# A four-layer decoder megakernel: five edits to the order of work in five of its stages

## What is computed

```python
# layer 0 feed-forward: gated sum of experts, each with a second bias
y = sum_e comb[:, e] * (gelu(h @ fc1[e] + b1[e]) @ fc2[e] + b2[e])
# layer 1 feed-forward: experts 0 and 1 have W = W + A @ B for gate, up and down
y = sum_e wt[:, e] * ((silu(h @ Wg[e]) * (h @ Wu[e])) @ Wd[e])
# layer 2 cross attention: q = rope(h @ Wq @ w_kc_q) @ W_qr ..., 16 heads
# layer 2 feed-forward: each token goes through one of 32 masked ternary matrices
# layer 3 attention, 16 heads of 128 nope and 64 rotary dimensions
q = rms(h @ Wq_a) @ Wq_b;  q_rope = rope(q[..., 128:])
score = (q_nope @ (Wk^T latent) + q_rope @ k_rope) / sqrt(192) + causal
out = softmax(score) @ latent, then folded with Wkv_b's value part and Wo
```

## Time and profile before

| what | value |
|---|---|
| median of three runs | 1622.96 us |
| the profiled execution's own time | 1620.76 us |
| its span, first to last instruction | 1619.0 us |
| granted TensorE clock, mean | 0.915 |
| TensorE matmul busy | 1356.9 us (84%) |
| VectorE busy | 828.8 us (51%) |
| ScalarE, GpSimd busy | 527.8 us (33%), 262.5 us (16%) |
| layer 0 feed-forward, start | 352.9 us |
| layer 1 feed-forward, start | 636.7 us |
| layer 2 cross attention, feed-forward, start | 918.6 us, 1189.7 us |
| layer 3 attention, start | 1287.4 us |

### The profile page before, as it was taken

The page is one execution under the profiler, slowest core; times in us unless marked ns, Lnnn a source line. Parts: engine busy times, 40 slices in busy tenths (PEclk is TensorE's granted clock), DMA queues, the critical chain, the costliest instruction groups (busy, mean ns, idle before and its releaser), DMA issues. The chain is left out here.

```text
span 1619.0 us, 28010 instructions
## 1 busy us (share of the span) xinstructions
PE 1356.9 (84%) x11687; PEld 1035.0 (64%) x11705; DVE 828.8 (51%) x1530; ACT 527.8 (33%) x967; POOL 262.5 (16%) x219
## 2 busy tenths in 40 slices
PE   5768996989999979799968888999748578978888
PEld 2348994557867667688847666787647444547555
DVE  4844435553253642433428546777345359981552
ACT  1331223562334652312223411223414413442451
POOL 0143422000120000111010113333010113320200
PEclk9868998988999989899978899999878799899999
DMA  3000001126014001000092240000056200000000
GB/s 100 1 1 4 4 4 54 53 63 137 0 35 142 1 1 30 1 1 1 1 241 82 79 141 1 1 1 1 1 166 215 87 8 1 1 0 1 28 1 26
DMA packets 83468, 69.41 MB, mean 43 GB/s; under 512 B 23752, under 2 KB 81552, under 8 KB 83216
## 3 DMA queue, kind: packets, MB, share of 16 engines
q1 hardware_dynamic: 82576, 65.53, 14.1%
q0 software_dynamic: 768, 2.10, 0.4%
HBM read 55.29 MB, written 12.32 MB: 42 GB/s over the span
## 5 line engine op out<-in xcount | busy, mean ns | idle before, releaser
L1158 PE MATMUL ps<-fixed,work 128*128 128x256 f32 x384 | 92.7, 392 | 20.5 <-DVE weights L1188 18.7
L1702 PE MATMUL ps<-rounded 128*128 128x512 f32 x384 | 96.3, 408 | 9.4 <-POOL rounded L1725 6.1
L637 PE MATMUL ps<-work,weights 128*128 128x256 f32 x384 | 89.3, 395 | 7.4 <-ACT weights L656 7.4
L1158 PEld LDWEIGHTS ps<-fixed,work 128*128 128x128 f32 x384 | 71.5, 193 | 35.9 <-DVE weights L1188 25.1
L1702 PEld LDWEIGHTS ps<-rounded 128*128 128x128 f32 x384 | 74.0, 195 | 29.4 <-issue 9.6
L637 PEld LDWEIGHTS ps<-work,weights 128*128 128x128 f32 x384 | 75.9, 199 | 19.3 <-ACT weights L656 8.3
L1207 POOL TENSOR_TENSOR fixed<-fixed,weights 128x768 f32<-128x768 f32 x32 | 58.0, 1811 | 148.3 <-DVE weights L1188 148.3
L1386 PE MATMUL ps<-work,weights 96*128 96x512 f32 x128 | 65.8, 641 | 12.4 <-DVE work L1409 10.4
L1725 POOL TENSOR_TENSOR rounded<-weights,rounded 128x256 fp32r<-128x256 f32 x32 | 22.9, 735 | 276.8 <-ACT rounded L1729 276.8
L656 ACT COPY weights<-ps 64x512 f32<-64x512 f32 x96 | 55.6, 579 | 25.8 <-PE ps L615 24.1
L1630 DVE SCALAR_TENSOR_TENSOR fixed<-ps,work,fixed 128x256 f32<-128x256 f32 x64 | 28.0, 479 | 65.5 <-PE ps L1563 65.5
(11 more groups left out here) (447 smaller groups left out, 3044.4 us busy)
## 6 DMA issues: line engine op xcount, KB each, us to landing
weights<-in_L_ffn_masksT SPq DMA_DIRECT2D x32, 256.0 KB, 5.6
sorted_in<-work SPq DMA_DIRECT2D x1, 4992.0 KB, 16.8
work<-sorted_in SPq DMA_DIRECT2D x13, 384.0 KB, 3.9
sorted_out<-work SPq DMA_DIRECT2D x13, 384.0 KB, 2.8
weights<-in_L_ffn_fc_w SPq DMA_DIRECT2D x16, 256.0 KB
weights<-in_L_xattn_Wq SPq DMA_DIRECT2D x2, 2048.0 KB, 10.0
weights<-in_L_xattn_WoT SPq DMA_DIRECT2D x2, 2048.0 KB, 10.4
weights<-in_L_ffn_Wg SPq DMA_DIRECT2D x8, 256.0 KB, 5.7
```

The source lines that it names most:

```text
L637: last = nc.tensor.matmul(ps[:, (0, 1, 4, 5)[j // 2], (j % 2) * D:(j % 2 + 1) * D], t.ctxT[:, u, j * P:(j + 1) * P], t.pm[:, u, :], start= ...
L1158: last = nc.tensor.matmul(seen[:, a, :], qf[:, c, u, a, :], k.hT[:, c, part * D:(part + 1) * D], start=c == 0, stop=c == KC - 1)
L1702: last = nc.tensor.matmul(ps[:, 2 * (n % 2) + i, :], a[:, q % 2, i, c, :], b[:, c, half * BANK:(half + 1) * BANK], start=c == 0 and part = ...
```

## The change

1. `project` waits in parts: tile 0 for the first sine operation of unit v-1, tile 1 for nothing, tile 2 for all three. `first_products` alternates between the two heads of a pair, so that neighbouring products use other rows and columns of the array and another PSUM bank.
2. Layer 3 attention: a unit is half of the tokens of a pair of heads, 16 in all. The rotary rows of both heads are one projection to bank 0, the nope rows of both another to bank 1. VectorE does three operations per unit, on 128, 64 and 64 rows. GpSimd does four additions of 32 rows per unit, three of them to other partitions than they read, and waits also for ScalarE's copies. Lag 3. GpSimd sorts the rotary weights with four copies in block 1. Four more DMAs.
3. The folds of layer 3 attention move into the layer 2 feed-forward, between the ranks and the first sorted block, behind 36 `hold` matmuls and a wait for the next stage's weights. ScalarE does the copies. Ten `hold` matmuls take their place.
4. Layer 1 feed-forward: experts in the order 2 to 7, 0, 1. Low-rank products in two parts: 4 first, 8 behind the first expert's products. ScalarE waits for the additions only before the last four halves.
5. Layer 0 feed-forward: the transposes of `comb` and the biases come behind expert 1's first products.

```diff
 def first_products(g):
-    for i in range(4):
-        p, e = divmod(i, 2)
-        for rows, width, first, tile in (...):
+    for p in range(2):
+        for tile, apart, at_row, width, first in ((0, 64, 0, 64, 0), (1, 64, 0, 64, 96), (2, 32, 0, 32, 64), (2, 32, 64, 32, 160)):
+            for e in range(2):
+                r, to = slice(64 * e, 64 * e + 64), at_row + apart * e
...
 def project(pe, v):
-    if v:
-        pe.wait_ge(s["sined"], 3 * v)
     for a in range(3):
+        if v and a != 1:
+            pe.wait_ge(s["sined"], 3 * v - 2 if a == 0 else 3 * v)
...
 # layer 3 attention, block 1
+@block.gpsimd
+def _(pool):
+    pool.wait_ge(w.sem, w.loaded)
+    for e in range(2):
+        for n in range(2):
+            nc.gpsimd.tensor_copy(to[:, :, :, n, e, :], of[:, :, :, e, n, :]).then_inc(s["sorted"], 1)
 # block 2: the loop over four fold groups and its copies on ScalarE and VectorE are gone
+hold(k, 6, 10)
 # block 3
+def projected(pe, v, kind, made):
+    u, tok = place(v)
+    for a in range(2):
+        last = nc.tensor.matmul(ps[:, 1 - kind, :], (w.nope, rot)[kind][:, a, u, :], qnT[:, a, tok], start=a == 0, stop=a == 1)
+    last.then_inc(s[made], 1)
+def rotated_rows(pe, v):
+    if v:
+        pe.wait_ge(s["sined"], 2 * v)
+    projected(pe, v, 1, "r_proj")
+def other_rows(pe, v):
+    if v:
+        pe.wait_ge(s["q_top"], 2 * v)
+    projected(pe, v, 0, "n_proj")
+def act_q(act, v):
+    act.wait_ge(s["n_proj"], v + 1)
+    if u >= 2:
+        act.wait_ge(s["scored"], 2 * u - 2)
+    for e in range(2):
+        nc.scalar.copy(qb[0:64, 2 * (u % 2) + e, tok], ps[64 * e:64 * e + 64, 1, :]).then_inc(s["q_top"], 1)
+def dve_q(dve, v):
+    dve.wait_ge(s["r_proj"], v + 1)
+    if v >= 2:
+        dve.wait_ge(s["q_ready"], v - 1)
+    nc.vector.tensor_tensor(by_seq(cs[:, v % 2, :]), by_seq(ps[:, 0, :]), bc(w.ropeT[:, 0, :], 1, 8), ALU.mult).then_inc(s["cosed"], 1)
+    for to, of in ((slice(0, 64), slice(64, 128)), (slice(64, 128), slice(0, 64))):
+        nc.vector.tensor_tensor(by_seq(sn[to, v % 2, :]), by_seq(ps[of, 0, :]), bc(w.ropeT[of, 1, :], 1, 8), ALU.mult).then_inc(s["sined"], 1)
+# GpSimd, for v in range(NH): waits cosed v + 1, sined 2 * v + 2, q_top 2 * v + 2, then
+    for e in range(2):
+        for half in range(2):
+            made = slice(64 * half + 32 * e, 64 * half + 32 * e + 32)
+            last = nc.gpsimd.tensor_tensor(qb[64 + 32 * half:96 + 32 * half, 2 * (u % 2) + e, tok], cs[made, v % 2, :], sn[made, v % 2, :], ALU.add)
+    last.then_inc(s["q_ready"], 1)
+attend(..., {"pe": rotated_rows, "pe_b": other_rows, "act": none, "act_b": act_q, "dve": dve_q,
+             "ready": lambda h: 2 * (h // 2) + 2}, 192 ** -0.5, causal=k.causal, turned=False, lag=3)
...
 # layer 0 feed-forward
-                if e == 0:
+                if e == 1:
                     pe.wait_ge(s["comb"], 1)
...
 # layer 1 feed-forward
+    TURN, LOW = (2, 3, 4, 5, 6, 7, 0, 1), (0, 4, 12)
+            low_rank(0)
             pe.wait_ge(s["h_rest"], KC)
...
+                if e == 0:
+                    pe.wait_ge(s["lowed"], 2)
+                    low_rank(1)
+                if e == 1:
+                    pe.wait_ge(s["lowed"], 6)
...
 # layer 2 feed-forward, TensorE, behind the ranks; ScalarE copies nope and pm of each g
+            hold(k, 4, 36)
+            pe.wait_ge(k.next.sem, k.next.loaded)
+            for g in range(4):
+                fold_nope(g)
+                fold_out(g)
+            pe.wait_ge(s["noped"], 4)
+            pe.wait_ge(s["pms"], 4)
             turn(0)
```

More of the change, by code:

```diff
@@ L1219, in load_L3_attn @@
     d, eng, r = k.dram, k.nc.sync, w.region
-    w.nr = r.take(2, NH, P, rows=96)
+    w.nope = r.take(2, NH // 2, P, rows=96)
+    w.pm = r.take(NH // 2, D)
     w.all = r.take(KC, 384)
@@ L1226, in load_L3_attn @@
     w.wo = r.take(NH, D)
+    w.rot = r.take(2, NH, DH, rows=96)
     w.rope = k.fixed.take(2, DH)
@@ L1253, in stage_L3_attn @@
     qnT = k.work.take(2, TOK, rows=96)
+    rot = k.work.take(2, NH // 2, P, rows=96)
     ss = k.work.take(2, NT)
     rstd = k.work.take(2, NT)
-    qb = k.work.take(3, TOK)
+    qb = k.work.take(4, TOK)
     sn = k.work.take(2, BANK)
@@ L1261, in stage_L3_attn @@
     kr = qb[:, 2, :].rearrange("p (a d) -> p a d", d=DH)
-    with k.stage("lat", "sq", "mean", "std", "rstd", "qn", "km", "kvn", "kra", "krb") as (block, s):
+    with k.stage("sorted", "lat", "sq", "mean", "std", "rstd", "qn", "km", "kvn", "kra", "krb") as (block, s):
         @block.tensor
@@ L1306, in stage_L3_attn @@
     lat = qb[0:64, 1, :]
-    with k.stage("vzero", "t_qn", "t_km", "c_qn", "c_km", "c_lat", "t_kv", "nope", "noped", "pm", "pms", "kvs") as (block, s):
+    with k.stage("vzero", "t_qn", "t_km", "c_qn", "c_km", "c_lat", "t_kv", "kvs") as (block, s):
         @block.tensor
@@ L1375, in stage_L3_attn @@
     w.region.at = w.mark
[L1376 to L1384, removed]
-            for a in range(2):
-                last = nc.tensor.matmul(ps[:, v % 2, :], w.nr[:, a, h, :], qnT[:, a, tok], start=a == 0, stop=a == 1)
-            last.then_inc(s["q_proj"], 1)
-        def act_q(act, v):
[L1390 to L1393, removed]
-            nc.scalar.copy(qb[0:64, h % 3, (v % 2) * BANK:(v % 2 + 1) * BANK], ps[0:64, v % 2, :]).then_inc(s["q_top"], 1)
-        quarters = (slice(64, 96), slice(96, 128))
-        def dve_q(dve, v):
-            h = v // 2
-            dve.wait_ge(s["q_proj"], v + 1)
-            if h >= 3:
-                dve.wait_ge(s["scored"], h - 2)
-            nc.vector.tensor_tensor(qb[hi, h % 3, (v % 2) * BANK:(v % 2 + 1) * BANK].rearrange("p (b t) -> p b t", t=SEQ),
-                                    ps[hi, v % 2, :].rearrange("p (b t) -> p b t", t=SEQ), bc(w.ropeT[hi, 0, :], 1, 8),
-                                    ALU.mult).then_inc(s["cosed"], 1)
@@ L1925, in copy_turned @@
                 nc.scalar.copy(sortedT[:, b % TURNED].rearrange("p c t -> p (c t)"), ps[:, b % 4, 0:KC * P]).then_inc(s["sortedT"], 1)
+            for g in range(4):
+                act.wait_ge(s["nope"], g + 1)
+                nc.scalar.copy(k.next.nope[:, :, 2 * g:2 * g + 2, :],
+                               ps[0:96, 2 + g % 2, :].rearrange("p (a i d) -> p a i d", a=2, i=2)).then_inc(s["noped"], 1)
+                act.wait_ge(s["pm"], g + 1)
+                nc.scalar.copy(k.next.pm[:, 2 * g:2 * g + 2, :].rearrange("p a d -> p (a d)"), ps[:, g % 2, :]).then_inc(s["pms"], 1)
             copy_turned(0)
@@ L2948, in decoder @@
             start_loads(n + 1)
+            k.next = loads.get(n + 1)
             rounded = ROUNDED_COLS.get(layer, 0)
```

125 lines of the change are left out of this document (65 added, 60 removed).

## The result

The changed kernel takes 1583.25 us (median of four, 1579.01 to 1589.24) beside 1621.74 us for the kernel before on the same chip: a ratio of 0.9754, with a 95% interval of 0.9729 to 0.978. The forecast was 1572 in a range of 1560 to 1590. The profiled execution took 1586.03 us, with a span of 1583.5, so 35.5 us less than the span before; 50.2 were forecast.

What follows compares the result with a forecast made beforehand. In the two attention loops neither engine fills the time; TensorE waits for VectorE in layer 2, and VectorE is never idle in layer 3. Terms 5 + 9 + 16.5 + 8.2 + 0.7 + 4.8 + 6 = 50.2 gave 1572 us, range 1560 to 1590.

Steps and rivals of the forecast that it cites:

- The start-up step of 4.5 us: Layer 2's attention loop: with the wait split, a start-up unit takes 4.5 us instead of 5.42; six such units save 5.5.
- Afterwards GpSimd stands next in line: Layer 2's loop after start-up: GpSimd's addition (1.82 us) becomes the next wait, 10.25 us per head against 10.83.
- VectorE's share: Layer 3's loop: VectorE loses 4.22 us per head and gains 2.1, so busy time falls from 8.0 to 5.9.
- the addition's price: Layer 3's loop: a GpSimd addition of 32 rows to other partitions costs 1.26 us, following columns; bounds 1.0 and 2.5.
- an addition takes over 1.6 us: Layer 3's loop: a GpSimd addition above 1.6 us was named as a sign that the prediction is wrong.
- today the first four blocks run at 1.2 GHz: Layer 2's feed-forward: the sorted blocks' transposes would start 0.9 us late but run at 2.4 GHz, net gain 0.7.
- Rival (c): Layer 2's feed-forward: clock stays low over the holds, fold ends late, 6 to 9 us lost: 1580; chance 0.13.
- biases at 2.4 GHz 16 x 0.21 = 3.4: Layer 0's feed-forward: behind expert 1, the 16 bias passes run at full clock and take 3.4 us, ending at 375.8.
- the lower end: Layer 0's feed-forward: gain of only 3 us instead of 6 if the clock falls in the copy's gap.
- (a): Layer 3's loop: GpSimd's shifted additions cost 1.5 to 2.2 us each and bound it, 1577 to 1620; chance 0.11.
- VectorE's 127.55 us: Layer 3's loop: VectorE's busy time now, divided by 16 heads to give 8.0 us per head.
- 0.99 us "beside nothing": VectorE's normalising product: 0.99 us with nothing beside it, against 1.81 beside GpSimd's addition in layer 2's loop.

Runs made afterwards that it cites:

- the second profile: The changed kernel profiled again with no edit: ratio 0.9756 to the kernel before, its profiled execution 1575.21 us.
- the filled kernel: The changed kernel plus unread products in TensorE's gaps in both grouped attention stages and layer 0's feed-forward: 1576.35 us, ratio 0.970.

## Why the prediction came out as it did

The total lay in the range and 11 us above the forecast. The stretches of the parts gave nearly the forecast sum, in part by luck: part 1b gave 3.5 us more than its term and part 5 3.5 less. By its steps:

- **Part 1a** (5): 4.4 in the profile after, 4.7 in the second one. Right; undoing it restores 2.33 us per 32 loads.
- **Part 1b** (9): 12.5, and 13.7 alone. Mechanism right, size wrong. The start-up step of 4.5 us came as worked out. What failed is "Afterwards GpSimd stands next in line": I had laid the addition end to end with the unit's own projection, but the next projection stands between, 2.46 us against the addition's 1.82, so next to nothing is left to wait for. The trace before could have told it.
- **Part 2** (16.5): 15.3. VectorE's share, the addition's price (1.26 when beside nothing, as taken; 1.34 in the mean) and the loop's length (123.0 against 121.8) held. What the sum did not have is GpSimd's wait for ScalarE's copies, 6 to 7 us at lag 3 and 28.6 at lag 2. It stayed small here only because of lag 3. The sign "an addition takes over 1.6 us" was met by the additions that start beside L694 (up to 1.70), not by the mean.
- **Part 3** (8.9): 8.4 and 8.1. Right in sum. Of "today the first four blocks run at 1.2 GHz" the gain came (from the first sorted transpose to the next stage 64.2 us in place of 65.9), but the 36 holds had no part in it: without them it is 64.2 too. Rival (c) did not happen: the clock rose to 1.00 by 1189, 3 us into the holds.
- **Part 4** (4.8): 5.0 and 5.7. Right.
- **Part 5** (6): 2.5 up to expert 2, and nothing by the start of layer 1's feed-forward between profiles whose first grouped stage is alike. The step "biases at 2.4 GHz 16 x 0.21 = 3.4" came true in the second profile (3.39) and not in the first (4.73). What failed in both is the silent next step, that all behind them then runs at 2.4 GHz: in either profile 6.8 us went at 1.2 GHz, which costs about 3.4 us more than at 2.4 GHz (an estimate from the clock alone), and 6.1 - 3.4 is near the 2.5 measured. The reason that I gave for the lower end, the gap of the copy, is not needed, as the filled kernel shows.
- **The sum** took every unchanged stage at its time in the one profiled execution. The two grouped stages can be 6 us longer in another, and that execution had both short; other stages move by 2 to 5 us. All unchanged stretches together cost 12.6 us in the profile after; the medians contain some of it. The prediction's range has no term for this. That the median stayed inside is owed to the room left for rivals that did not come, (a) and (c) above all.

Two readings of the prediction were wrong. VectorE's 127.55 us belong to a window of 175 us, not to the loop, where it was busy for 117.66, so 7.4 us per head and not 8.0; the 2.1 us per head that it was to lose came (2.2). And L694 does not take 0.99 us "beside nothing". It takes 0.69 there, as in all 16 heads of layer 1's loop, where GpSimd adds nothing. The 0.99 were already beside L1420, and beside L1207 it is 1.51 in most heads.

The rule of the Trainium skill (GPSIMD Engine Reference, section 2.1) by which a core starts the next instruction once its own share is done gave nothing here: eight additions in a row took 11.30 us, 1.41 each. With the sharing of interfaces that section 8 of the same page of the Trainium skill states, for VectorE instructions of two SBUF inputs, this trace agrees: an addition of 1.26 us takes up to 1.70 when it starts beside L694, and L694 up to 1.30 in place of 0.69. It stayed as hidden as taken: L694 is at 0.91 us in the mean in layer 3's loop, where it was at 0.94 before.

## What to carry to other kernels

Before an addition, copy or wait is priced, draw the ring that it stands in: here one needless wait for a copy cost 6 us at lag 3 and 28.6 at lag 2, and with it in place the pipeline depth decided whether the change was a gain at all. When a group's mean lies above the price of its like, look at the single instructions and their neighbours before you call it the price of the form. When a forecast is summed from one execution, look first for stages with a clock that can go either way, and state them as a spread of their own; and follow a gain of a few us to the end of the next stage or two, as it may be gone there. Filler products earn their place only where a run without them is slower; 36 of them earned nothing here.

## What was not expected of the hardware

In the filled kernel the granted clock fell to 0.50 at about 375.3 us, though TensorE's matmuls had left no gap since 358.8; it fell while TensorE made the last of 16 products of 8 contraction rows. An addition by GpSimd whose output lies on other partitions than its inputs costs what any of 512 columns costs, 1.26 us; beside VectorE's product of two SBUF inputs it takes 1.59 to 1.70. The same stage of the same kernel takes 79.5 or 85.9 us, depending on whether the clock falls again in its first 10 us. And 2.5 us gained in one stage were lost in the next through the clock, so that both orders came to 277.5 us.
